# Orders, table loads and first transfers of a two-stream decoder kernel

## What is computed

```
x = _layernorm(x + _L0_attn_ref(x, W_qkv, W_out), axis=-1)      # linear attention, softmax features
x = _layernorm(x + _L0_xattn_ref(x, ctx, Wq, Wkv, Wout, bout))  # softmax attention, 16 heads, context + own keys
x = _layernorm(x + _L0_ffn_ref(x, gate_w, ..., w1, w2, w3, ...))# experts, silu, top 2, and a shared one
x = _layernorm(x + _L1_attn_ref(...))   # decayed linear attention, then a norm of its own
x = _layernorm(x + _L1_xattn_ref(...))  # softmax attention, 16 heads of 64
x = _layernorm(x + _L1_ffn_ref(...))    # 8 experts of 512, gelu (tanh form)
x = _layernorm(x + _L2_attn_ref(...))   # linear attention, then a gelu feed-forward
x = _layernorm(x + _L2_xattn_ref(...)); x = _layernorm(x + _L2_ffn_ref(...))
x = _layernorm(x + _L3_attn_ref(...));  x = _layernorm(x + _L3_xattn_ref(...))
x = _layernorm(x + _L3_ffn_ref(x, weight, bias))   # ternary weights, quantised input
```

## Time and profile before

| | kernel before |
|---|---|
| median of three runs | 1081.8 us |
| profiled execution, its own time | 1080.39 us |
| its span in the trace | 1078.4 us |
| TensorE (PE) busy | 921.6 us, 85% |
| weight loads (PEld) busy | 687.3 us, 64% |
| VectorE (DVE) busy | 570.5 us, 53% |
| ScalarE (ACT) busy | 440.2 us, 41% |
| GpSimd (POOL) busy | 47.4 us, 4% |
| mean granted TensorE clock | 0.93 |

### The profile page before, as it was taken

How to read it: one execution, slowest core, us unless ns; L and a number is a source line. 1 busy time by engine, 2 the same in 40 slices (tenths; PEclk the granted TensorE clock), 3 DMA queues, 4 the chain that set the end, 5 groups by cost and what they waited for, 6 DMA issues and landing times. The chain is left out here.

```text
span 1078.4 us, 20461 instructions
## 1 busy us (share of the span) xinstructions
PE 921.6 (85%) x8328; PEld 687.3 (64%) x8328; DVE 570.5 (53%) x1589; ACT 440.2 (41%) x897; POOL 47.4 (4%) x68
## 2 busy tenths in 40 slices
PE   6689899899988898988778978988998888898782
PEld 4246578778877584666426745876888766784441
DVE  5744535654356376364554864665425458364347
ACT  2036415354554462361224333533355553632332
POOL 0300000000010000000000000001001000000000
PEclk9699979999999998995969999999999999999875
DMA  9000000301001101121000000030100110000000
GB/s 336 27 2 1 2 2 1 157 2 36 1 18 57 76 1 40 41 88 55 1 1 12 1 2 2 2 156 2 35 2 19 60 73 2 1 1 1 1 1 19
DMA packets 6829, 35.97 MB, mean 33 GB/s; under 512 B 721, under 2 KB 4305, under 8 KB 5458
## 3 DMA queue, kind: packets, MB, share of 16 engines
q1 hardware_dynamic: 6738, 34.68, 8.7%
HBM read 34.15 MB, written 0.52 MB: 32 GB/s over the span
## 5 line engine op out<-in xcount | busy, mean ns | idle before, releaser
L660 PE MATMUL bank<-xT,weights_F 128*128 128x256 f32 x832 | 201.9, 386 | 0.7 <-DVE small L1285 0.7
L660 PEld LDWEIGHTS bank<-xT,weights_F 128*128 128x128 f32 x832 | 152.5, 193 | 23.6 <-issue 4.3
L668 PEld LDWEIGHTS bank<-weights_F,p 128*128 128x128 f32 x1088 | 133.9, 192 | 16.8 <-issue 5.6
L668 PE MATMUL bank<-weights_F,p 128*128 128x128 f32 x1088 | 140.6, 278 | 3.2 <-ACT p L1890 2.3
L1742 ACT ACTIVATE p<-bank 128x512 f32<-128x512 f32 x160 | 84.0, 602 | 115.4 <-PE bank L506 101.4
L1330 DVE SCALAR_TENSOR_TENSOR res<-bank,comb,res 128x128 f32<-128x128 f32 x184 | 55.9, 345 | 74.7 <-PE bank L668 72.5
L1814 ACT ACTIVATE p<-bank 128x512 f32<-128x512 f32 x72 | 42.9, 598 | 99.1 <-PE bank L660 98.6
L1171 DVE TENSOR_REDUCE m_wide<-bank 128x4 f32<-128x512 f32 x96 | 60.3, 683 | 43.1 <-PE bank L767 35.3
L1346 DVE TENSOR_TENSOR p<-p,bank 128x512 f32<-128x512 f32 x72 | 49.3, 685 | 49.1 <-PE bank L660 26.8
L1890 ACT ACTIVATE p<-bank 128x512 f32<-128x512 f32 x64 | 36.5, 598 | 44.6 <-PE bank L660 44.5
L1179 DVE TENSOR_REDUCE mx<-bank 128x4 f32<-128x512 f32 x64 | 39.9, 682 | 27.8 <-PE bank L500 27.6
(11 more groups left out here) (323 smaller groups left out, 1441.5 us busy)
## 6 DMA issues: line engine op xcount, KB each, us to landing
weights_F<-in_L1f SPq DMA_DIRECT2D x2, 4096.0 KB, 13.2
weights_F<-in_L0f SPq DMA_DIRECT2D x2, 3456.0 KB, 13.1
weights_F<-in_L2f SPq DMA_DIRECT2D x2, 3456.0 KB, 11.4
weights_Y<-in_L1x_kv SPq DMA_DIRECT2D x2, 1024.0 KB, 10.3
weights_Z<-in_L1x SPq DMA_DIRECT2D x2, 1024.0 KB, 11.3
weights_Y<-in_L2a SPq DMA_DIRECT2D x2, 898.0 KB, 4.5
weights_Z<-in_L2x SPq DMA_DIRECT2D x2, 449.0 KB, 3.5
weights_L3m<-in_L3m SPq DMA_DIRECT2D x2, 288.0 KB, 6.2
```

Of the source, the lines that this page charges most:

```text
L660: m = mm(b[:, k * NT:(k + 1) * NT], W[weight][:, f:f + P], s.xT[:], start=True, stop=True)
L668: m = mm(b[:, tk(u)], h[:, tk(u)], w, start=k == 0, stop=k == len(chunks) - 1)
```

## The change

Five things are changed.

1. The orders of PE, DVE, ACT and POOL in `TURN_ORDER` are new; SP's is the same.
2. A helper `use(functions)` asks for a table set when another is in, and silu, both gelus and `exp_ln` go through it. The request stands ahead of the waits of the step. In L2a it moves ahead of the wait on the weights.
3. SP's first loads are `xT` of pair 0, the weights of L0a, the constants, `xT` of pair 1. Both `ctx_tok` loads go behind all the weights.
4. The spreading of the bias rows leaves the head of pair 1. It becomes three steps on PE, two on DVE and one on ACT, in stream b, behind the `o` step of its L0a. Its intermediate goes to `kT` and no longer to `qT`.
5. The first waits are narrower: PE no longer waits for constants and masks at its head but for the constants at the transpose of L0a and for the masks (three, the other two are dropped) at L0x. The clearing of `vz` moves from DVE to POOL, ahead of POOL's first steps. The unused `warm` goes.

```diff
-        "a3 b1 a2 b1 a2 b3 a2 b2 a4 b1 a1 b1 a2 b1 a1 b1 a1 b1 a1 b1 a1 b1 a1 b1 a2 b1 a6 b1 a15 b1 a3 b2 a3 b1 "
+        "a1 b1 a2 b1 a2 b1 a2 b4 a1 b1 a1 b2 a2 b2 a1 b1 a2 b1 a2 b2 a1 b1 a1 b2 a1 b1 a1 b1 a1 b1 a3 b1 a5 b1 "
...
+                    pe.wait_ge(*weights("con"))
                     b = opened("act", "L0a", "qsT")
...
+                    if pair == 1:
+                        rows = lambda a, e: s.p[0:1].rearrange("p a b -> p (a b)")[:, a:e]
+                        pe.wait_ge(*weights("rows"))
+                        b = opened("act", "rows", 2)
...
+                        yield
+                        filled(mm(opened("dve", "rows", 0)[:], ones_row, rows(0, 512), start=True, stop=True), "rows", 0)
+                        yield
+                        b = opened("dve", "rows", 1)
...
                     pe.wait_ge(*freed("L0x", "qk"))
+                    pe.wait_ge(S("masks"), 3)
...
-            pe.wait_ge(*weights("con"))
-            pe.wait_ge(S("masks"), 5)
...
-            for s in streams:
-                dve.memset(s.vz[:], 0.0).then_inc(S(f"zeroed_{s.g}"), 1)
...
+            def use(functions):
+
+                if table[0] != functions:
+                    act.preload_act_table_set(functions)
+                    table[0] = functions
...
-                        table[0] = "silu"
+                        use("silu_and_others")
                         b = bank(st, "gate", e)
...
-                                table[0] = "gelu_tanh"
+                                use("gelu_apprx_tanh_and_others")
...
+                    use("gelu_and_others")
                     act.wait_ge(*weights("L2a", turn))
-                    act.preload_act_table_set("gelu_and_others")
-                    table[0] = "gelu"
...
+            for s in streams:
+                pool.memset(s.vz[:], 0.0).then_inc(S(f"zeroed_{s.g}"), 1)
...
-            load("con")
             load_input(0, "xT", 0)
             load("L0a")
+            load("con")
+            load_input(1, "xT", 1)
             load_input(0, "ctxT", 0)
```

More of the change, by code:

```diff
@@ L146 @@
     "pe":
[10 rows of a table removed]
-    "dve":
[9 rows of a table removed]
-    "act":
[8 rows of a table removed]
[11 rows of a table added]
+    "dve":
[10 rows of a table added]
+    "act":
[8 rows of a table added]
     "pool":
-        "a1 b1 a1 b2 a3 b1 a1 b1 a1 b1 a2 b1 a2 b2 a1 b2 a1 b1 a2 b1 a4 b4 a1 b2 a1 b1 a1 b1 a1 b1 a2 b1 a2 b3 a1 "
-        "b1 a1 b2 a2 b2 a1 b1 ",
+        "b1 a2 b2 a3 b2 a1 b1 a3 b1 a2 b3 a1 b1 a1 b2 a2 b2 a4 b4 a1 b1 a1 b1 a1 b1 a1 b1 a4 b3 a1 b1 a1 b2 a2 b2 "
+        "a1 b1 ",
     "sp":
@@ L181 @@
 }
-WARM = {"a": "", "b": ""}
 def build(nc, dram, out):
@@ L222, in _build @@
     neg_causal_t_bf = sb("neg_causal_t_bf", [P, P], BF16)
-    ones_bf = sb("ones_bf", [P, P], BF16)
-    zeros_bf = sb("zeros_bf", [P, P], BF16)
     ones_row = const("ones")[0:1, 0:128]
@@ L419, in _ @@
             mm, tr = pe.matmul, pe.transpose
-            def warm(b, n):
-                for _ in range(n):
-                    mm(heads(b[:], 4), ident_bf[:], among(zeros_bf[:], 4), start=True, stop=True)
             def program(g):
@@ L428, in program @@
                 key = pair = turn = None
-                warmth = iter(WARM["ab"[g]].split())
                 def opened(by, *a):
-                    b = ring.open((pair, *a), by)
-                    warm(b, int(next(warmth, 0)))
-                    return b
+                    return ring.open((pair, *a), by)
                 def filled(ins, *a):
@@ L596, in L0a @@
                     yield
+                    if pair == 1:
+                        rows = lambda a, e: s.p[0:1].rearrange("p a b -> p (a b)")[:, a:e]
+                        pe.wait_ge(*weights("rows"))
+                        b = opened("act", "rows", 2)
+                        for k in range(2):
+                            m = mm(b[:, k * D:(k + 1) * D], rows(896 + k * D, 896 + (k + 1) * D), ones_row, start=True, stop=True)
+                        filled(m, "rows", 2)
+                        yield
+                        filled(mm(opened("dve", "rows", 0)[:], ones_row, rows(0, 512), start=True, stop=True), "rows", 0)
+                        yield
+                        b = opened("dve", "rows", 1)
+                        mm(b[:, 0:384], ones_row, rows(512, 896), start=True, stop=False)
+                        pe.wait_ge(*ready("small"))
+                        pe.wait_ge(*ready("L3a"))
+                        pe.wait_ge(*freed("rows", 2))
+                        mm(b[:, 128:256], s.kT[:, 0:T], W["L2x_o"], start=False, stop=False)
+                        filled(mm(b[:, 256:384], s.kT[:, T:2 * T], W["L3a_o"], start=False, stop=True), "rows", 1)
+                        yield
                     pe.wait_ge(*ready("L0x"))
@@ L1063, in program @@
                     pair = STREAMS * turn + g
[L1064 to L1079, removed]
                     for stage in (L0a, L0x, L0f, L1a, L1x, L1f, L2a, L2x, L2f, L3a, L3x):
@@ L1239, in L0a @@
                     yield
+                    if pair == 1:
+                        o.count(dve.tensor_copy(biases[:, 0:4].rearrange("p n d -> p (n d)"), bank("rows", 0)[:]), free("rows", 0))
+                        yield
+                        o.count(dve.tensor_copy(biases[:, 4:7].rearrange("p n d -> p (n d)"), bank("rows", 1)[:, 0:384]), free("rows", 1))
+                        yield
                     keep_values("L0x", "vc")
@@ L1657, in program @@
                     pair = STREAMS * turn + g
-                    if pair == 1:
-                        o.count(dve.tensor_copy(biases[:, 0:4].rearrange("p n d -> p (n d)"), bank("rows", 0)[:]), free("rows", 0))
-                        o.count(dve.tensor_copy(biases[:, 4:7].rearrange("p n d -> p (n d)"), bank("rows", 1)[:, 0:384]), free("rows", 1))
                     for stage in (L0a, L0x, L0f, L1a, L1x, L1f, L2a, L2x, L2f, L3a, L3x):
@@ L1666, in program @@
                             yield from ternary_weights()
-            for s in streams:
-                dve.memset(s.vz[:], 0.0).then_inc(S(f"zeroed_{s.g}"), 1)
             dve.wait_ge(*weights("con"))
-            for dst, src in ((ident_bf, IDENT), (neg_causal_bf, const("neg_causal")), (neg_causal_t_bf, const("neg_causal_t")),
-                             (ones_bf, const("ones"))):
+            for dst, src in ((ident_bf, IDENT), (neg_causal_bf, const("neg_causal")), (neg_causal_t_bf, const("neg_causal_t"))):
                 dve.tensor_copy(dst[:], src).then_inc(S("masks"), 1)
-            dve.memset(zeros_bf[:], 0.0).then_inc(S("masks"), 1)
             take_turns("dve", program)
@@ L1681, in _ @@
             table = [None]
+            def use(functions):
+                if table[0] != functions:
+                    act.preload_act_table_set(functions)
+                    table[0] = functions
             def exp_ln():
-                if table[0] != EXP_LN:
-                    act.preload_act_table_set(EXP_LN)
-                    table[0] = EXP_LN
+                use(EXP_LN)
             def program(g):
@@ L1776, in L0a @@
                     yield
+                    if pair == 1:
+                        keep("rows", 2, s.kT)
+                        yield
                     keep("L0x", "kc", s.kcT)
@@ L2003, in program @@
                     pair = STREAMS * turn + g
-                    if pair == 1:
-                        keep("rows", 2, s.qT)
                     for stage in (L0a, L0x, L0f, L1a, L1x, L1f, L2a, L2x, L2f, L3a, L3x):
@@ L2195, in _ @@
             load_input(0, "x_tok", 0)
-            load_input(0, "ctx_tok", 0)
             load("small")
@@ L2200, in _ @@
                          dram["rows"][0:1]).then_inc(loaded["rows"], 16)
-            for name in ("xT", "x_tok", "ctxT", "ctx_tok"):
+            for name in ("x_tok", "ctxT"):
                 load_input(1, name, 1)
@@ L2210, in _ @@
             load("L3f")
+            for g in range(STREAMS):
+                load_input(g, "ctx_tok", g)
             _, a, e = GROUPS["L1a"]["L1a_bb"]
```

## The result

The changed kernel takes 1056.6 us (median of four runs, 1055.18 to 1059.5), the kernel before 1081.9 us beside it. The ratio is 0.9762 [0.9727, 0.9797]: 2.4% faster, where 0.8% was forecast, and 1.4 us under the low end of the range. The profiled execution took 1055.18 us with a span of 1052.8 us. A few executions of the later runs were in a slower state of the chip; medians and ratios leave them out. The line is the page's busy line of the changed kernel.

The account below looks back on a forecast made before the run. PE was taken as the bound, with small idle gaps to win. The span 1078.4 - 4 (start) + 0 (requests) + 1 (switches) - 6 (orders) = 1069.4 us gave a median of 1072.8 us, 0.8% faster, range 1058 to 1090 us.

Parts of the forecast that it names:

- What bounds the kernel: Whole kernel: PE bounds it, busy 921.6 of 1078.4 us; 113.1 us of its idle time are small gaps an order can win.
- The start: First loads and L0a: earlier first matmul -1.7 us, bias rows moved behind b's `o` -2.3 us; -4 us, between -8 and +1.
- Asking for tables ahead: ACT's silu and gelu loads: already ahead of the waits, so earlier requests give 0 to 1.7 us of ACT; taken as 0.
- Six more switches: ACT, in L1f and L2a: six more table loads, 7.7 us of ACT, mostly in idle time; +1 us, bounds 0 and +7.7.
- The orders: All engines' new strings: fill PE's small gaps; -6 us, a twentieth of 113 us, effect between 3.5 and 35 us of either sign.
- Gaps that meet: Rival, chance 0.20: both L0x at the change of turns and both L3a in the first turn meet, +14.4 us; 1093.2 us.
- Orders worth nothing: Rival, chance 0.21: old and new orders equally good to within 0.7 us per length; 1078.8 us.
- Tables on the path: Rival, chance 0.04: silu and gelu loads delayed PE, up to 47.5 us could go; with half of it and the start 1054.1 us.
- What would show it: Signs: first matmul at about 5.2 us, 83 loads, PE idle about 9 us less; wrong if both L0x idle over 16 us.

Follow-up runs that it names:

- new_orders: The kernel before with only the new strings of PE, DVE, ACT and POOL, without the steps of the bias rows: 1057.3 us, 0.9761.
- old_orders: The changed kernel with the old strings and the steps of the bias rows set in, so all of the change but the new orders: 1082.1 us, 0.9984.
- start_only: The kernel before with SP's new sequence of first transfers, the narrower first waits and `vz` cleared on POOL, nothing else: 1076.4 us, 0.9939.
- use_only: The kernel before with only the table requests of silu and both gelus, `use(...)`, ahead of the banks: 1082.2 us, 1.0004.
- ahead: The changed kernel with the exp and ln table request ahead of the bank wait in the inverses, L1x denominators and L2a: 1055.1 us, 0.9771.
- first_new: The changed kernel with the new strings only up to a's L2x of pair 0 and the old ones from there: 1078.2 us, 0.9972.
- no_switch: The changed kernel with silu and both gelus replaced by the identity, so one table load is left of 83: 1042.3 us, 0.9612.
- last_old: The changed kernel with the old strings from the start of a's L2x of pair 2 on: 1067.0 us, 0.9875.
- l3x_old: The changed kernel with the old strings only in the last L3x (from the start of L3x of pair 2): 1065.5 us, 0.9859.
- tail_old: The changed kernel with the old strings from b's L3a of pair 3 on: 1066.3 us, 0.9873.

## Why the prediction was wrong

**What bounds the kernel: right.** The gain is idle time of PE in small gaps: 23.5 of 25.6 us of span, with the busy time the same.

**The start, -4 us: steps off, worth not settled.** The first matmul is at 3.89 us and not 5.2, released by a transfer as said; the L0a weights took 2.7 and not 4.0 us from issue to landing. The constants landed 4.5 us behind their issue and not 3.5, so ACT's tables came at 6.17 us, not 5.2. With the moved rows it is worth 0.7 us (`new_orders` against the changed kernel) or 1.7 us (`old_orders`, up to 4.8 by its interval), and without them `start_only` gives 6.6 us. The -4 us is neither shown nor excluded. L0x begins 4.5 us earlier in the changed kernel (24.63 against 29.18 us), and 1.2 us earlier with the old strings (27.96 us in `old_orders`): most of it is the new order.

**Asking for tables ahead, 0: right** (`use_only` 1.0004, `ahead` inside the spread).

**Six more switches, +1 us: within its bounds.** The count of 83 came true. What the six cost by themselves no run shows. As an estimate, by the dearest price measured, 0.79 per us, they cost 6.1 us (7.7 x 0.79); by the cheapest 1.1 us. The prediction's bounds of 0 and 7.7 us hold either.

**The orders, -6 us: this is the step that failed.** They are worth 24 us (`new_orders`, `old_orders`). The mechanism was named and the sign was right; the term was too small by a factor of four. The yardstick was the mean of both streams between the ends of L1a and L2x in the two turns, 194.3 against 193.65 us. From it came the 0.7 us per length that pulled the value toward the low end. Two turns that agree show only that the two old orders are equally good there. They bound nothing about a third order: the same length is 191.2 us in the first turn of the changed kernel and 185.6 in the second. Nor does the mean of the ends measure progress: it was ahead by 20.6, 23.7, 8.8 and 16.9 us at the four places, and by 25.6 us at the end. The bound of 35 us stood in the text, but the low end of the range used 16 us.

A better pointer lay in PE's waits, which I read and did not size: 17.6 us of PE waiting for exponentials of an engine that is idle 59% of the time, of which 16.0 us went. It points at the right size, but it is no safe sum. `first_new` removed 5.8 us of these waits and gave 1.3 to 4.0 us (by ratio and by median), with PE idle as long as before. And a wait can move: the gap of 5.5 us before the gates of the last L3x went, but one of 6.3 us came before the gates of b's first L3x, so this wait is 7.1 us in all and was 6.4.

**Gaps that meet, 0.20: refuted, and the gap is another one.** The two L0x at the change of turns idle 9.8 us in 56, less than the 14.3 us in 54 from which the rival was priced. The 4.8 us that PE is busy less in 486 to 594 us come with the gap at L3x, which no rival named. In 594 to 756 us PE is busy 10.8 us more; the rival did not price that, although its own last sentence named it. The two L3a stand side by side in the first turn from about 447 to 469 us, and PE idles 4.2 us there. That is 1.9 us in ten, as in the second turn before (1.8 in ten from 970 to 1014 us). The rival's stretch for the latter, 970 to 1024 us, ran on into the last L3x: 3.6 of its 11.45 us lie behind 1014 us, most of them in the gap before the gates.

**Orders worth nothing, 0.21: refuted** by `new_orders`. **Tables on the path, 0.04: refuted** by `use_only`. Its time, 1054.1 us, is the one nearest to the result, by chance only: `no_switch` shows 14.3 us for all loads together, where the rival took 23.7 us from half of 37 of them.

**What would show it.** PE did not idle over 16 us in the two L0x at the change of turns, and of the gaps of over 2 us that were to name DVE's maxima one stands there, 2.07 us before L481. Such gaps did not grow over the kernel (L488 7.2 us, before 8.0; L481 fell more). The loss in the first 27 us fell from 8.3 to 6.6 us, said 6. The clock stayed at 0.93. PE idle fell by 23.5 us, said 9.

## What to carry to other kernels

When a fixed order of steps is searched anew, start from the bounding engine's waits: those that name an engine with time to spare are what an order can remove, though a removed wait may come back behind another engine. How far two existing orders differ says little. A bad pairing of stages must be priced together with the pairing that it makes later. Where two streams start the same stage together and its first products leave the matmul engine without work, try to let one go some us ahead: the gap costs its own length and then slower products behind it, here 4.0 and 7.9 us. The changed kernel still has such a gap, of 6.3 us, in the first turn (at 504.64 us); no run with the new middle piece is without it.

## What the hardware did that I had not expected

- After the same gap of 5.5 us the products of L3x ran at the lower rate (2.08 instead of 1.13 us for four) for some 4 us in the kernel before, some 10 us in `old_orders` and `last_old`, and some 20 us in `l3x_old` and `tail_old`. The length of the gap alone does not set what follows.
- A table load on a half idle engine is not free when it is added (0.60 to 0.79 us per us) and nearly free to keep (0.14 us per us when removed). If the order of the steps was searched with the loads in it, that could be the reason; no run shows it.
- A transfer of 256 KB landed 2.7 us after its issue when it stood ahead of the 564.5 KB of constants and 4.0 us when it stood behind them; the constants took 4.5 and not 3.5 us in turn.
